# Cross-attention and mixture of experts on one Trainium2 core: raw scores from small products without padded keys, q of two pairs first, and filler products

## The chip, the cores and the metric

The kernel runs on one core of a Trainium2 chip. The metric is the device time of one launch in microseconds; lower is better. All times in this text are in microseconds unless marked ns. Engines: PE is TensorE (PEld its weight loads), DVE is VectorE, ACT is ScalarE, POOL is GpSimd, SP is SyncE, which here issues nearly all DMAs.

## The reference

Sixteen sequences of 256 tokens and width 128 attend to 64 context rows each, with 16 heads of 8. The softmax is unusual: it runs over the heads, not over the keys. Then comes a feed-forward part with two shared experts and eight routed ones, of which each token takes two.

```python
xn = layernorm(x)
q, k, v = xn @ Wq.T, ctx @ Wk.T, ctx @ Wv.T            # 16 heads of 8
scores = einsum('bhqd,bhkd->bhqk', q, k) / sqrt(8)
attn = softmax(scores, axis=1)                          # over the 16 heads
x = x + einsum('bhqk,bhkd->bhqd', attn, v) @ Wo.T
h = layernorm(x)
x = x + h + shared(h) + sum over the top 2 of 8 experts of gate * expert(h)
```

## The kernel before

The 16 sequences are 8 pairs. Attention works in 16 units: unit u is one half (128 queries of each of the two sequences) of pair u // 2. Groups of four units are a body of code (`four_units`), with k = u % 4. The scores of a unit fill four PSUM banks, [128 = 2 sequences x 64 keys, 16 heads x 128 queries]. One unit, engine by engine, each engine in its own program order:

- PE: `raw_scores` (L1337), the products of k and q; then, of earlier units, the output projection (`project_out`, L1368); `minus_max` (L1346), which subtracts the maximum over heads by a product with a negative identity; `weighted_values` of unit u-2 (L1356); then `prologue_rest`, which for the first eight units holds q products (`project_q`, L1309) and transposes (`transposes`, L1298) of later pairs; from unit 9 on transposes for the feed-forward part (L1415).
- DVE: `max_heads` (L922), `sum_heads` of unit u-1 (L927, L930), `low_q` (L860), the addition of the attention result (L934), statistics of the second norm, and at k = 3 the seed of its inverse root (L912 to L917).
- ACT: `exps` (L674), two exponentials for half of the heads each, a copy of the values (L667), and its own `prologue_rest`: first norms (L588), copies of transposes (L594), `high_q` (L600), weights rounded to 16 bits (L565, L572) and scaled (L573), and spreading V (L608).
- POOL: `normalise` (L452), `low_part` (the rests of the rounded weights, L437), `inverse_deviation` (L465), `ffn_inputs` (L476).

Four semaphores tie a unit together: raw_ready, max_ready, s_ready, exp_done. `raw_scores` of the next unit overwrites the banks and so waits for the exponentials, half by half.

Precision: q and k are split into a 16-bit high and low part each. `project_q` makes q of a pair in PSUM, `high_q` and `low_q` write the two parts to `qs`, SyncE stores them to `q_rows` in DRAM (`store_q`, L302) and loads them back spread over the partitions (`load_q`, L314, two DMAs of 64 partitions each for a pair). `kRep` holds, in the same way, both parts of k. In a product over all four combinations of parts a head needs 32 rows.

In this kernel `raw_scores` uses the full array: for each head one product of 128 rows and 128 columns of weights. The weights come from `kPad`, in which all but the head's own rows and the sequence's own keys are zero. GpSimd zeroes kPad once (L403), and SyncE fills it for each pair with 16 DMAs of 8 KB from `kRep` (`pad_k`, L298). kPad has two buffers, so the pad of pair p waits until pair p-2 has been read. The SyncE queue holds in program order: context and x, weight parts 0 to 2, wo (16 small ones), centroids and bias (L317, L318), pad of pair 0 mixed with store and load of q of pairs 0 and 1, weight parts 3 and 4, pad of pair 1, store and load of pairs 2 and 3, then for each further pair a pad, a store and a load, at the end the last two pads.

Ahead of unit 0 stand the q products of pairs 0 to 3. The products of V (`project_v`, L1282) stand behind the raw scores of unit 0, and its copy (L638) in unit 0's ACT code. q of pairs 4 to 7 is made in units 2, 4, 5 and 6 on PE and its low part in units 3, 5, 6 and 7 (`LOW_UNITS`) on DVE. A pair above 3 has bank 7 for its q, so `project_q(pair)` waits for qlo_ready >= pair, the low parts of all pairs below it.

## Time and profile before

| | |
|---|---|
| median of 3 runs | 435.03 us (434.7 to 436.25) |
| the profiled execution's own time | 433.28 us |
| its span, first to last instruction | 431.5 us |
| granted TensorE clock, mean over the span | 0.902 |
| PE / DVE / ACT / POOL busy | 74% / 73% / 65% / 64% |

The attention units take about 32 to 165 us of the span; the feed-forward part follows. A busy share is a mean over parts with different limits. The span leaves out 1.8 us around the first and the last instruction. Granted clock 1.0 is 2.4 GHz, 0.5 is 1.2 GHz.

### The profile page before, as it was taken

How to read it: one execution, taken by the hardware profiler on the slowest of the kernel's cores; microseconds unless marked ns; L12 is line 12 of the kernel's file. 1: busy time of each engine (PE TensorE's matmuls, PEld its weight loads, DVE VectorE, ACT ScalarE, POOL GpSimd, SP SyncE). 2: the span in 40 equal slices, each digit the busy share in tenths (PEclk: the TensorE clock that was granted, in tenths of full speed). 3: DMA queues.
4: the chain of work that ended last, by engine and by line, in shares of the span. 5: the costliest groups of instructions: out<-in, count | busy, mean ns of one | idle time of the engine just before them, and what ended most of it. 6: DMA issues, size and time to landing. Idle time of an engine off the chain costs nothing.

```text
span 431.5 us, 11459 instructions
## 1 busy us (share of the span) xinstructions
PE 319.6 (74%) x3780; PEld 245.9 (57%) x3781; DVE 314.3 (73%) x628; ACT 282.4 (65%) x530; POOL 275.3 (64%) x275
## 2 busy tenths in 40 slices
PE   5456577566767749669887899879999999999400
PEld 1235254344545437347654576669898998989300
DVE  7767778799799995995859856636666666766257
ACT  3675688577578663558876488637676676767265
POOL 8530877589788793077867776606777676777700
PEclk9968599999699875999999899969999999999955
DMA  8838512312300000011111250131323322231087
GB/s 269 277 95 290 153 35 59 81 39 56 82 12 9 2 0 3 0 51 51 46 37 51 82 130 24 46 100 44 99 77 87 91 71 80 73 99 55 8 329 255
DMA packets 37850, 37.18 MB, mean 86 GB/s; under 512 B 13860, under 2 KB 32935, under 8 KB 37296
## 3 DMA queue, kind: packets, MB, share of 16 engines
q1 hardware_dynamic: 33264, 28.18, 22.7%
q0 software_dynamic: 4544, 8.44, 6.0%
q8 instruction: 26, 0.43, 0.4%
q14 instruction: 16, 0.13, 0.1%
HBM read 21.74 MB, written 14.72 MB: 84 GB/s over the span
## 4 chain that ended last, share of the span: by engine, by line
PE 35%; DVE 18%; POOL 15%; issue 14%; SPq 8%; ACT 4%; DMA 4%; POOLq 1%; DVEq 0%; ACTq 0%
SPq L298 5%; POOL E L452 5%; POOL results L532 4%; DVE E L999 4%; PE banks L1543 3%; PE banks L1545 3%; PE banks L1544 3%; PE banks L1558 3%; PE banks L1557 3%; PE banks L1559 2%; PE banks L1475 2%; PE banks L1337 2%; PE banks L1479 2%; PE banks L1477 2%; DVE X L1245 2%
## 5 line engine op out<-in xcount | busy, mean ns | idle before, releaser
L532 POOL DMA_INDIRECT results<-E,qRep x78 | 86.3, 1107 | 44.5 <-issue 27.7
L522 POOL DMA_INDIRECT gathered<-xs,slot x64 | 68.4, 1068 | 41.2 <-issue 18.6
L1216 DVE TENSOR_TENSOR E<-hid,E 128x512 f16<-128x512 f32 x78 | 54.0, 692 | 38.2 <-ACT E L790 37.2
L452 POOL TENSOR_TENSOR E<-E,rZ 128x1024 f32<-128x1024 f32 x32 | 68.3, 2160 | 16.9 <-DVE rZ L930 16.9
L788 ACT ACTIVATE hid<-banks 128x512 f32<-128x512 f32 x78 | 46.8, 601 | 44.0 <-PE banks L1545 25.5
L1475 PE MATMUL banks<-wprojL,E 128*128 128x128 f16 x256 | 46.8, 221 | 15.4 <-DVE E L999 15.3
L750 ACT ACTIVATE hid<-banks 128x512 f32<-128x512 f32 x64 | 38.6, 604 | 29.1 <-PE banks L1461 26.0
L1557 PE MATMUL banks<-wprojL,E 128*128 x312 | 56.1, 219 | 1.8 <-issue 0.9
L999 DVE TENSOR_TENSOR E<-hid,E 128x512 f16<-128x512 f32 x64 | 45.8, 734 | 15.2 <-ACT E L751 14.7
L1559 PE MATMUL banks<-wprojH,E 128*128 x312 | 55.7, 219 | 0.0
L1558 PE MATMUL banks<-wprojH,E 128*128 x312 | 55.7, 219 | 0.0
L674 ACT ACTIVATE E<-banks 128x1024 f32<-128x1024 f32 x32 | 33.1, 1095 | 26.6 <-PE banks L1346 26.6
L922 DVE TENSOR_REDUCE Mx<-banks 128x128 bf16<-128x2048 f32 x16 | 36.7, 2292 | 18.3 <-PE banks L1337 18.3
L790 ACT ACTIVATE E<-banks 128x512 f16<-128x512 f32 x78 | 47.1, 603 | 0.0
L1477 PE MATMUL banks<-wprojH,E 128*128 128x128 f16 x256 | 46.6, 220 | 0.0
L1479 PE MATMUL banks<-wprojH,E 128*128 128x128 f16 x256 | 46.6, 220 | 0.0
L1543 PE MATMUL banks<-qRep,wfcH 128*128 128x256 f16 x156 | 43.6, 280 | 0.5 <-ACT E L790 0.5
L1545 PE MATMUL banks<-qRep,wfcH 128*128 128x256 f16 x156 | 43.5, 279 | 0.0
L1544 PE MATMUL banks<-qRep,wfcL 128*128 128x256 f16 x156 | 43.5, 279 | 0.0
L1475 PEld LDWEIGHTS banks<-wprojL,E 128*128 128x128 f16 x256 | 25.2, 98 | 29.7 <-DVE E L999 24.7
L751 ACT ACTIVATE E<-banks 128x512 f16<-128x512 f32 x64 | 38.4, 601 | 0.0
L927 DVE TENSOR_REDUCE Z<-E 128x128 f32<-128x2048 f32 x16 | 36.4, 2276 | 0.0
(205 smaller groups left out, 833.4 us busy)
## 6 DMA issues: line engine op xcount, KB each, us to landing
qRep<-gathered SPq DMA_DIRECT2D x39, 129.0 KB, 2.2
qRep<-q_rows SPq DMA_DIRECT2D x16, 256.0 KB, 3.9
qRep<-results SPq DMA_DIRECT2D x8, 512.0 KB, 7.0
X<-in_x SPq DMA_DIRECT2D x4, 512.0 KB, 6.3
kPad<-kRep SPq DMA_DIRECT2D x128, 8.0 KB
q_rows<-qRep SPq DMA_DIRECT2D x8, 256.0 KB, 2.3
out<-X SPq DMA_DIRECT2D x8, 256.0 KB, 3.9
xs<-in_wproj_t SPq DMA_DIRECT2D x1, 1536.0 KB, 8.8
```

The lines of the kernel that those rows point to most:

```text
L452: g.tensor_tensor(heads, heads, rZ[:, k % 2, :].unsqueeze(1).unsqueeze(3).broadcast_to([P, HH // 2, P, 2]), ALU.mult).then_inc(attn_ready, 1)
L522: g.indirect_dma_start(out=gathered, out_offset=bass.IndirectOffsetOnAxis(ap=slot[:, k, i:i + 1], axis=0), in_=xs[:, i, :], in_offset=None ...
L532: g.indirect_dma_start(out=results, out_offset=bass.IndirectOffsetOnAxis(ap=xg[:, k, h, 2 * D:ROW].bitcast(I32), axis=0), in_=yg[:, k, h, ...
L999: v.tensor_tensor(hidL[:, i % 2, c], hid[:, c], hidH[:, i % 2, c], ALU.subtract).then_inc(hlo_ready, 1)
L1475: t.matmul(o, hidH[:, e, c, tok], wprojL[:, e, f], start=(e == 0 and c == 0 and q == 0), stop=False, skip_group_check=True)
L1477: t.matmul(o, hidH[:, e, c, tok], wprojH[:, e, f], start=False, stop=False, skip_group_check=True)
L1543: t.matmul(o, wfcH[:, e, f], xgT[:, j, 1], start=True, stop=False)
L1544: t.matmul(o, wfcL[:, e, f], xgT[:, j, 0], start=False, stop=False)
L1545: last = t.matmul(o, wfcH[:, e, f], xgT[:, j, 0], start=False, stop=True)
L1557: t.matmul(o, gH[:, j, c, tok], wprojL[:, e, f], start=(c == 0), stop=False)
L1558: t.matmul(o, gH[:, j, c, tok], wprojH[:, e, f], start=False, stop=False)
L1559: last = t.matmul(o, gL[:, j, c, tok], wprojH[:, e, f], start=False, stop=(c == FC - 1))
```

## The change

1. kPad, its zeroing and all its 128 DMAs go. `raw_scores` takes kRep and qRep directly: for each head and sequence a product of 32 rows and 64 columns of weights, 32 products for a unit instead of 16. A head's 32 rows and the sequence's 64 output partitions select one tile of the array; products for the two sequences alternate. For this, the order of rows in kRep (`select`) and in qRep (`load_q`, now four DMAs of 32 partitions with a stride of 4) changes, and the exponentials read their banks in another order.
2. Only pairs 0 and 1 have their q made ahead of unit 0. Pair u+1 has its q products in unit u (1 to 6), pair u+2 its transposes in unit u (0 to 5), pair u its low part in unit u (2 to 7). Everything from pair 2 on uses banks 6 and 7, with the same waits as pairs above 3 had. On DVE the inverses 2 and 3 go behind the first maximum. On ACT the weight copies are dealt out anew (all four of part 2 in unit 0).
3. The products of V stand ahead of unit 0, into banks 0 and 1, and ACT copies V behind its first four weight copies. PE waits for that copy ahead of unit 0.
4. `keep_going(count)`: products of the identity with itself into a bank part that nobody reads. 20 of them ahead of unit 0, and 6 behind the raw scores of units 0, 1 and 2.

```diff
-            def pad_k(pair, lo=0, hi=PAD_PARTS):
-
-                j = pair % 2
-                if pair > 1:
-                    sp.wait_ge(raw_ready, 2 * pair - 2)
-                for i in range(lo, hi):
-                    r = slice(DK * i, DK * i + DK)
-                    sp.dma_start(kPad[r, j, i % 2, :, i // 2 % 2], kRep[r, pair]).then_inc(kPad_loaded[j], 16)
-
...
-                src = q_rows[pair].rearrange("l (r g) n -> (l r) (g n)", g=QUARTER)
-                for i in range(2):
-                    sp.dma_start(qRep[64 * i:64 * i + 64, pair].rearrange("p g q -> p (g q)"), src
-                                 ).then_inc(q_loaded[pair], 16)
+                for l in range(2):
+                    src = q_rows[pair, l].rearrange("(r g) n -> r (g n)", g=QUARTER)
+                    for i in range(2):
+                        sp.dma_start(qRep[2 * i + l:P:4, pair].rearrange("p g q -> p (g q)"), src
+                                     ).then_inc(q_loaded[pair], 16)
...
-            sp.wait_ge(masks, BASICS + 2)
-            for side in range(2):
-                sp.wait_ge(spread_out[side], 2)
-            pad_k(0, 0, 4)
-            store_q(0, 0)
-            pad_k(0, 4, 6)
-            store_q(0, 1)
-            pad_k(0, 6, 9)
-            load_q(0, 0)
-            pad_k(0, 9)
-            load_q(0, 1)
+            for j in range(2):
+                store_q(0, j)
+            for j in range(2):
+                load_q(0, j)
             for part in range(3, 5):
                 load_weights(part)
...
-            then(g.memset(kPad_flat, 0.0))
...
+            act.wait_ge(masks, BUILT)
+            for i in range(2):
+                act.wait_ge(v_ready, i + 1)
+                s.activation(V[:, 4 * i:4 * i + 4], v_ps[i], ACT.Copy).then_inc(V_ready, 1)
             deviation(1)
+            act.wait_ge(V_ready, 2)
+            spread_v(0, 0)
+            first_norm(2)
...
+                if 0 < u < PAIRS - 1:
+                    high_q(u + 1)
+                if u < PAIRS - 2:
+                    copy_xnT(u + 2)
+                if 0 < u < PAIRS - 3:
+                    first_norm(u + 3)
                 if u == 0:
+                    highs(2, 0, 4)
...
-                    if (first or second) and u in LOW_UNITS:
-                        low_q(4 + LOW_UNITS.index(u))
+                    if second or first and k > 1:
+                        low_q(u)
...
             def project_v():
-                pe.wait_ge(xnT_ready, 4)
+                pe.wait_ge(spread_out[0], 2)
...
+            project_v()
             pe.wait_ge(masks, BUILT)
 
+            def keep_going(count):
+
+                for _ in range(count):
+                    t.matmul(y_ps[:, 0:P], ident[:], ident[:], start=True, stop=True)
+
             def prologue_rest(u):
+                if 0 < u < PAIRS - 1:
+                    project_q(u + 1)
+                if u < PAIRS - 2:
+                    transposes(u + 2)
...
-                for i in range(4):
-                    if not first and i % 2 == 0:
-                        pe.wait_ge(exp_done, 2 * u + i // 2 - 1)
-                    for h in range(4 * i, 4 * i + 4):
-                        at = 2 * (h // 2 % QUARTER) + h // HH
-                        last = t.matmul(scores[:, i, P * (h % 4):P * (h % 4) + P],
-                                        kPad[:, k // 2, h % 2, h // 2].rearrange("p b s -> p (b s)"),
-                                        qRep[:, pair, at, P * (k % 2):P * (k % 2) + P],
-                                        start=(h % 4 == 0), stop=False, skip_group_check=True)
+
+                for i in range(2):
+                    if not first:
+                        pe.wait_ge(exp_done, 2 * u + i - 1)
+                    for odd in range(2):
+                        for g in range(QUARTER):
+                            at = 2 * g + i
+                            for b in range(2):
+                                r = slice(GRP * (2 * b + odd), GRP * (2 * b + odd) + GRP)
+                                last = t.matmul(scores[64 * b:64 * b + 64, 2 * i + odd, P * g:P * g + P],
+                                                kRep[r, pair, QUARTER * i + g],
+                                                qRep[r, pair, at, P * (k % 2):P * (k % 2) + P],
+                                                start=(g == 0), stop=False, skip_group_check=True)
                 last.then_inc(raw_ready, 1)
...
+            pe.wait_ge(V_ready, 2)
...
-                    if first and k == 0:
-                        project_v()
+                    if first and k < 3:
+                        keep_going(6)
...
+            keep_going(20)
             four_units(0, True)
```

## Rows read from the trace of the kernel before

**Rows 1.** Waits: who waited for whom, us in total, times, longest

```profile
PE banks L1337 <- DMA kPad<-kRep: 9.0, 6, 2.3
```

**Rows 2.** Timeline of SyncE's queue: start, duration of the issues, line, count

```profile
15.41 0.43 SPq L318 DMA_DIRECT2D bias<-in_rbias  x1
...
30.35 1.15 SPq L314 DMA_DIRECT2D qRep<-q_rows  x2
...
65.70 12.10 SPq L298 DMA_DIRECT2D kPad<-kRep  x16
...
81.25 12.10 SPq L298 DMA_DIRECT2D kPad<-kRep  x16
```

**Rows 3.** Timeline of TensorE up to unit 0

```profile
14.80 1.95 PE L1309 MATMUL banks<-x,xs 128*64 128x256 f32 x16 [0.82 <-ACT x L594]
...
31.83 1.05 PE L1337 MATMUL banks<-qRep,kPad 128*128 128x128 f16 x16 [2.15 <-DMA kPad<-kRep]
32.72 3.38 PE L1282 MATMUL banks<-xs,x 128*128 128x128 f32 x16
```

**Rows 4.** Timeline of VectorE and TensorE, seed, end of GpSimd's stretch, unit 12

```profile
92.27 0.16 DVE L917 TENSOR_SCALAR rstd<-var 128x8 int32<-128x8 int32 x1
...
110.45 0.61 PE L1415 MATMUL banks<-ident,xs 128*128 128x128 f16 x8 [2.74 <-POOL xs L476]
...
126.49 2.29 DVE L922 TENSOR_REDUCE Mx<-banks 128x128 bf16<-128x2048 f32 x1 [0.42 <-PE banks L1337]
```

**Rows 5.** Timeline of VectorE: start, unit 0, units 6 and 7

```profile
17.42 0.69 DVE L860 TENSOR_TENSOR qRep<-banks,qRep 128x512 f16<-128x512 f32 x1 [0.17 <-ACT qRep L600]
...
35.13 2.49 DVE L855 SCALAR_TENSOR_TENSOR wfcL<-E,wfcH 128x512 f16<-128x512 f32 x4
...
80.24 2.29 DVE L922 TENSOR_REDUCE Mx<-banks 128x128 bf16<-128x2048 f32 x1 [2.40 <-PE banks L1337]
...
85.63 0.63 DVE L860 TENSOR_TENSOR qRep<-banks,qRep 128x512 f16<-128x512 f32 x1
...
88.53 2.29 DVE L922 TENSOR_REDUCE Mx<-banks 128x128 bf16<-128x2048 f32 x1 [0.51 <-PE banks L1337]
```

**Rows 6.** DMA issues: count, KB each, median us from issue to landing

```profile
qRep<-gathered SPq DMA_DIRECT2D x39, 129.0 KB, 2.2
...
q_rows<-qRep SPq DMA_DIRECT2D x8, 256.0 KB, 2.3
```

**Rows 7.** Timeline of ScalarE: weight copies, table, copies of V

```profile
17.28 2.17 ACT L565 ACTIVATE wfcH<-E 128x512 f16<-128x512 f32 x4
...
30.34 1.28 ACT L630 ACT_TABLE_LOAD   x1
...
38.80 1.11 ACT L638 ACTIVATE V<-banks 128x512 f32<-128x512 f32 x2
```

**Rows 8.** Windows, raw products' instructions alone: stretch, length, busy, PEclk, DMA, GB/s

```profile
18.00:20.00 2.00, 0.00 (x0) 0.00 (x0) 0.86 0.33 20
99.70:102.50 2.80, 1.08 (x16) 0.90 (x16) 1.00 0.10 12
```

**Rows 9.** Timeline of TensorE, units 5 to 7

```profile
77.36 0.66 PE L1298 MATMUL banks<-ident,xn 128*128 128x128 f32 x4
...
83.63 1.12 PE L1356 MATMUL banks<-E,vPad 128*32 128x128 f32 x32
86.40 1.08 PE L1309 MATMUL banks<-x,xs 128*64 128x256 f32 x8 [1.65 <-DVE qRep L860]
87.42 1.07 PE L1337 MATMUL banks<-qRep,kPad 128*128 128x128 f16 x16
88.33 1.11 PE L1368 MATMUL banks<-wo,oT 128*128 128x128 f32 x8
```

**Rows 10.** Timeline of TensorE and ScalarE in unit 6: subtraction, exponentials

```profile
82.68 1.02 PE L1346 MATMUL banks<-Mx,negI 128*128 128x512 bf16 x4 [1.53 <-DVE Mx L922]
...
83.37 2.06 ACT L674 ACTIVATE E<-banks 128x1024 f32<-128x1024 f32 x2 [2.12 <-PE banks L1346]
```

More of the change, by code:

```diff
@@ L94, in xattn_moe_kernel @@
         kRep = sb("kRep", [P, PAIRS, HH, SK], F16)
-        kPad = sb("kPad", [P, 2, 2, HH, 2, SK], F16)
+        spare = sb("spare", [P, 2 * ROW + 2 * 12 * TILES], F16)
         vPad = [sb(f"vPad{j}", [P, 2, HH * (GRP + DK)]) for j in range(2)]
@@ L135, in xattn_moe_kernel @@
         table = sb("table", [P, 2, -(-MAX_TILES // QUAD) * QUAD], I32)
-        kPad_flat = kPad[:].rearrange("p j o g b s -> p (j o g b s)")
-        padding = kPad_flat[:, 0:2 * ROW].rearrange("p (s r) -> p s r", s=2)
+        padding = spare[:, 0:2 * ROW].rearrange("p (s r) -> p s r", s=2)
         x2_flat = x2[:].rearrange("p l t -> p (l t)")
@@ L191, in xattn_moe_kernel @@
         k_ps = [banks[:, i, :] for i in (0, 1)]
-        v_ps = [banks[:, i, :] for i in (4, 5)]
+        v_ps = [banks[:, i, :] for i in (0, 1)]
         spread_ps = [[banks[:, 2 * i:2 * i + 2, :] for i in sides] for sides in ((1, 3), (0, 1))]
@@ L195, in xattn_moe_kernel @@
         q_ps = [banks[:, i, :] for i in (6, 7)]
-        t_in = [t_ps[0], t_ps[1], t_ps[0], t_ps[1]] + 4 * [banks[:, 6, :]]
-        q_in = [q_ps[0], q_ps[1], q_ps[0], q_ps[1]] + 4 * [banks[:, 7, :]]
+        t_in = t_ps + (PAIRS - 2) * [banks[:, 6, :]]
+        q_in = q_ps + (PAIRS - 2) * [banks[:, 7, :]]
         scores = banks[:, 0:4, :]
@@ L226, in xattn_moe_kernel @@
             sem(n) for n in ("xn_ready", "xn1_ready", "t_ready", "xnT_ready", "q_ready"))
-        kPad_loaded, vPad_ready = [sem(f"kPad_loaded{j}") for j in range(2)], sem("vPad_ready")
+        vPad_ready = sem("vPad_ready")
         raw_ready, max_ready, s_ready = sem("raw_ready"), sem("max_ready"), sem("s_ready")
@@ L674, in exps @@
                     s.activation(E[:, k, 4 * i:4 * i + 4].rearrange("p g q o -> p g o q"),
-                                 scores[:, 2 * i:2 * i + 2].rearrange("p b (g o q) -> p (b g) o q", o=2, q=P), ACT.Exp,
+                                 scores[:, 2 * i:2 * i + 2].rearrange("p o (g q) -> p g o q", q=P), ACT.Exp,
                                  scale=DK ** -0.5).then_inc(exp_done, 1)
@@ L820, in _ @@
             for low in range(2):
-                m = select[:, low].rearrange("p g (s i b x) -> p g s i b x", s=2, i=2, b=2)
+                m = select[:, low].rearrange("p g (b x s i) -> p g b x s i", s=2, i=2, b=2)
                 for i in range(2):
-                    last = v.tensor_copy(m[:, :, low, i], groups)
+                    last = v.tensor_copy(m[:, :, :, :, low, i], groups)
             last.then_inc(select_ready, 1)
@@ L886, in _ @@
             first_stats(3)
-            inverse(2)
-            inverse(3)
-            for pair in range(2, 4):
-                low_q(pair)
             def pair_stats(n, j):
@@ L1290, in transposes @@
                 pe.wait_ge((xn_ready, xn1_ready)[pair % 2], pair // 2 + 1)
-                if pair in (2, 3):
-                    pe.wait_ge(xnT_ready, pair - 1)
-                if pair == 4:
-                    pe.wait_ge(qlo_ready, 3)
-                if pair > 4:
+                if pair == 2:
+                    pe.wait_ge(qlo_ready, 1)
+                if pair > 2:
                     pe.wait_ge(xnT_ready, pair)
@@ L1302, in project_q @@
                 pe.wait_ge(xnT_ready, pair + 1)
-                if pair in (2, 3):
-                    pe.wait_ge(qlo_ready, pair - 1)
-                if pair > 3:
+                if pair > 1:
                     pe.wait_ge(qlo_ready, pair)
```

63 lines of the change are left out of this document (8 added, 55 removed).

## The prediction

> **What bounds the kernel now.** I read the page first, then the waits, then one timeline per engine over the 16 attention units, then the chain of waits around the places where an engine stood idle. Behind 165 us everything hangs on the end of attention, so I look only at how fast the units follow each other. A unit is a loop over three engines: 16 raw products on TensorE, a maximum on VectorE, four products that subtract it, two exponentials on ScalarE that free the scores' banks. Nothing of it is near full; each engine waits for the next. Two things hold it up besides. TensorE waits for kPad six times, 9.0 us [rows 1]: SyncE spends 12.1 us on the 16 small issues of one pair, and the following block begins 15.55 us behind it [rows 2]; the rest is the store and load of a later pair's q in the same queue. A pair of units can't be quicker than that. The first unit begins at 31.83 us, right behind the last pad of pair 0 [rows 3]. Later GpSimd holds: from the seed of the second norm (92.27 us) its stream runs almost without a gap through norm steps, two normalisations and four weight rests to the lower halves of pair 0, and TensorE has waited 2.74 us for these when it goes on at 110.45 us [rows 4].
>
> **The first unit.** What stays: the products of q end at 16.75 us [rows 3], its low half of pair 1 at 18.11 us [rows 5], SyncE is free at 15.84 us [rows 2]. So the stores go out at about 17.3 and 18.2 us. A store lands in 2.3 us [rows 6]; bulk loads still run, I take 20.0 us. The four loads of pair 0 take 4 x 0.58 us of SyncE (half of what one pair's two took, 1.15 us), to 22.3 us, and a load of their size lands in 2.2 us [rows 6]: 24.5 us. TensorE: the products of V move up to 16.75 us, 1.7 us at full clock (they took 3.38 us at the low one [rows 3]). ScalarE can copy V only behind its four weight copies, 19.45 us, and needs 1.1 us [rows 7]: 20.6 us. Then come the 20 products nobody reads. Each is as large as one of V's eight, which took 3.38/8 = 0.42 us at the low clock: 0.21 us at the full one, 4.3 us together, or 8.5 us if all run low. TensorE was idle from 16.75 us, and the granted clock, 0.86 over 18 to 20 us, had fallen before 20 [rows 8]; now it works until 18.4 us, and I take the clock as high or coming up soon: raw products at 25.5 us (25.1 if high at once, 26.7 if the first eight are slow). The later of the two, TensorE, sets it. ScalarE must not be late: its table load, now the last thing ahead of unit 0, ended at 31.6 us [rows 7]; 1.7 us come ahead of it (copies of V, the first spreading), four copies of 0.6 us of q and of transposes go behind, and so do about 1.9 us of waits for TensorE between them: about 29.1 us. The first exponential is due at 25.5 + 1.15 + 2.29 + 0.69 and the handoffs, 29.7 us, so this is hidden, by 0.6 us only. Gain at this point 31.83 - 25.5 = 6.3 us.
>
> **A raw product's new price.** 32 products of 128 columns by 32 rows and 64 keys stand for 16 full ones. If the two halves of the array run side by side, the time stays at 1.07 us [rows 9]. That products of 64 output rows run two by two, q shows: four of them with 256 columns each take 1.08 us, while V's eight at full width with 128 columns, 1024 columns as well, took 3.38 us at the low clock, 1.7 us at the full one [rows 3, 9]. And 32 records of products of 32 output rows take 1.12 us [rows 9]. The bound from below is no change (the same columns stream), from above twice, 2.0 us: either the pairs go one by one, or load and product of a tile stand in line (16 products 1.08 us and 16 loads 0.90 us [rows 8]). I take 1.15 us, by the nearest row (1.12) plus a new change of shape between transposes and raw products: raw products start 0.06 us before the q products end, but the full products of L1368, which have the shape that the raw ones had, start 0.16 us before those end [rows 9]. So about 0.1 us for a change.
>
> **Units 0 to 7.** The raw products of unit 0 end at 26.65. Maximum 2.29, subtraction to the last exponential 2.75 (0.69 until the first of the two starts, and 2.06 for both [rows 10]), then the second half of the raw products 0.6, and four handoffs: unit 1 ends its raw products at 32.5. VectorE has by then done both moved inverses (four small operations, about 0.8) and the four weight rests (2.5 [rows 5]). Six fillers, 1.3 us, lie under the 2.29 us maximum; if the clock were low they would be 2.6 us and stick out by 0.3. Unit 1: maximum to 34.8, subtraction, q of pair 2 (1.08), transposes (0.66 [rows 9]), raw products to 38.5; VectorE's sum and reciprocal end there too.
> From unit 2 on comes what I think most readers would overlook: all q share bank 7, and the low half of pair u is now made in unit u, behind maximum, sum and reciprocal, while TensorE's stream has the products of pair u+1, the transposes of pair u+2 and the raw products of unit u+1 queued behind the wait for it. Before, only units 5 and 6 had this. Unit 6 prices it: maximum at 80.24, low half 85.63, q products 86.40, raw 87.42, next maximum 88.53 [rows 5, 9]: 8.3 us, with transposes 8.9, and with the raw price of above 8.35 and 8.95. A unit without it takes about 6 to 7. Maximum 2 starts at 38.5, so does its low half at 43.9 and maximum 3 at 47.4; three units of 8.95 and one of 8.35 lead to maximum 7 at 82.7 us. It was at 88.53 [rows 5]. So of the 6.3 us 5.8 are left: all of SyncE's stalls go, and the new wait takes nearly as much back. The q of pairs 2 to 7 are needed two units or more behind their low half, some 9 us and more against 2.3 + 2.3 + 2.2 us of store, issues and load: hidden.
> Nothing else costs: ScalarE's copies per unit are under 8 us, GpSimd's normalisation and rests 6.5 us, the 3.6 us memset and SyncE's waits that go were covered.
>
> **Units 8 to 15.** The stretch from the seed to 110.45 us is GpSimd's own work, 18.2 us, and moves as it is: 5.8 us earlier. In unit 12 a wait for kPad goes, but VectorE idled only 0.42 us there [rows 4]: -0.4. Five raw products on the path (10 to 13, 15) cost 5 x 0.1 = +0.5. The rest, 165 us to the end, shifts.
> Sum: -5.8 - 0.4 + 0.5 = -5.7 us. The profiled execution has 433.28 us with a span of 431.5, and its own after would be 427.6; the median of the three runs is 435.03, so I say 429.3 us.
>
> **Rivals.** (A) Products of two halves don't overlap, or tile loads stand in line. For it: no row has 32-row tiles; against: all rows with column tiles overlap. 0.9 us more than 1.07 in 13 raw products on the path, instead of 0.1: +10.4 us, 439.7. The gain without any raw cost is 6.2 us and some units hide theirs; over 13 raw products it is gone at 0.5 us each. Chance 0.10. This one ends slower.
> The Trainium skill (TensorE: Matmul & The Clock Gate, Part 3: Packing small matmuls) says that a weight load overlaps running products only where the row groups differ. In this change a tile's next load has its own row group, which would give rival A's in-line price; the full-width raw products, one row group all of them, hid their loads here, so the trace doesn't bear the rule out for them, and no run yet shows small tiles.
> (B) The fillers run at the low clock or q lands late: raw products at 28.5 to 29.4 us, 3 to 3.9 us of the gain gone, 432.8. For it: the clock was low by 20 us, and V's products at 32.72 us were slow too [rows 3, 8]. Chance 0.11.
> (C) The clock falls in units 3 to 7, where TensorE has more gaps and no fillers: subtraction, q products, transposes and raw products take up to twice their 1.0, 1.1, 0.7 and 1.1 us, as V's did [rows 3], some 3 us per unit, five units: +15, 444. Against: units 5 and 6 had these gaps and the fast prices [rows 9]. Chance 0.05.
> (D) More gain: GpSimd's stretch shortens because the 1.1 us VectorE stall in the seed doesn't come, TensorE stays fast behind 110 us (its raw, subtraction and value products were slow there, 1 to 2.5 us), or the first unit is at 24.5. -9 us, 426. Chance 0.14.
> My forecast has 0.57, its own range 427 to 431.8; 0.03 is for what I don't see.
>
> **Numbers.** A measurement tells about 0.5% (2.2 us) from no change. Faster by more: 0.57 + 0.14 and 0.03 of B = 0.74. Within: the rest of B and the near side of others, 0.11. Slower: A and C, 0.15. The range 425.0 to 435.0 takes in forecast, B and most of D; A and C lie outside.
>
> **What would show it.** Right: first raw products at 25 to 27 us; they take 1.1 to 1.2 us; no idle time there behind a DMA; q products of units 2 to 6 released by the low half, 8.3 to 9 us between maxima; seed at about 86.5 us and the 18.2 us behind it unchanged. Wrong: raw products near 2 us, a first unit at 29, q products at twice their price in units 3 to 7, or a seed stretch that got shorter.

## The result, and the profile of the changed kernel

The changed kernel takes 428.31 us (median of 4 runs, 428.15 to 429.16), the kernel before 435.18 beside it (4 runs, 434.7 to 436.25): a ratio of 0.9843 with an interval of 0.982 to 0.9865. The profiled execution took 428.38 us with a span of 426.6; before it was 433.28 and 431.5. The forecast was 429.3, in a range of 425.0 to 435.0, faster with a chance of 0.74. It came true, and in the attention part by nearly the forecast amount (5.6 us instead of 5.7), but some of its terms were off and cancelled, which is luck. The rows show which. All ratios leave out slow executions (one of the kernel before with 438.82 us, one of a later kernel with 549.3 us at a mean granted clock of 0.558).

The timeline of SyncE's queue ahead of unit 0 (start, duration of the issues, line, count):

```profile
17.53 1.24 SPq L290 DMA_DIRECT2D q_rows<-qRep  x2
21.91 5.50 SPq L303 DMA_DIRECT2D qRep<-q_rows  x8
```

The view of the two stores' line over 15 to 30 us; its last row says how long a store took to land:

```profile
L290 SPq DMA_DIRECT2D q_rows<-qRep x2: 377/378/378, 17.5 to 18.4; - x2
...
DMA to landing us min/median/max: 3.8/4.1/4.4
```

The timeline of TensorE, up to unit 0 (against [rows 3]), then unit 2 with the raw products of unit 3, then units 5 and 6 (against [rows 9]), then the end of GpSimd's stretch (against [rows 4]):

```profile
16.94 2.05 PE L1237 MATMUL banks<-xs,x 128*128 128x128 f32 x16
20.83 4.70 PE L1276 MATMUL banks<-ident 128*128 128x128 f32 x40 [1.84 <-ACT V L596]
26.77 0.67 PE L1294 MATMUL banks<-qRep,kRep 32*64 32x128 f16 x32 [1.24 <-DMA qRep<-q_rows]
...
46.31 1.97 PE L1260 MATMUL banks<-x,xs 128*64 128x256 f32 x8 [0.57 <-DVE qRep L817]
48.21 1.12 PE L1251 MATMUL banks<-ident,xn 128*128 128x128 f32 x4
49.26 1.08 PE L1294 MATMUL banks<-qRep,kRep 32*64 32x128 f16 x32
...
73.60 1.08 PE L1260 MATMUL banks<-x,xs 128*64 128x256 f32 x8 [1.73 <-DVE qRep L817]
74.62 0.66 PE L1251 MATMUL banks<-ident,xn 128*128 128x128 f32 x4
75.20 0.67 PE L1294 MATMUL banks<-qRep,kRep 32*64 32x128 f16 x32
...
82.11 1.08 PE L1260 MATMUL banks<-x,xs 128*64 128x256 f32 x8 [1.65 <-DVE qRep L817]
83.12 0.67 PE L1294 MATMUL banks<-qRep,kRep 32*64 32x128 f16 x32
...
106.09 0.61 PE L1372 MATMUL banks<-ident,xs 128*128 128x128 f16 x8 [2.64 <-POOL xs L449]
```

The timeline of VectorE in unit 1, then in unit 6 with the maximum of unit 7 (against [rows 5]), and the seed:

```profile
33.16 2.29 DVE L875 TENSOR_REDUCE Mx<-banks 128x128 bf16<-128x2048 f32 x1 [0.32 <-PE banks L1294]
35.36 0.64 DVE L892 CAST centH<-cent 128x8 f16<-128x8 f32 x1
36.04 1.08 DVE L894 TENSOR_TENSOR centL<-cent,centH 128x8 f16<-128x8 f32 x1
37.04 2.27 DVE L880 TENSOR_REDUCE Z<-E 128x128 f32<-128x2048 f32 x1
39.35 0.95 DVE L883 RECIPROCAL rZ<-Z 128x128 f32<-128x128 f32 x1
40.22 2.23 DVE L875 TENSOR_REDUCE Mx<-banks 128x128 bf16<-128x2048 f32 x1
...
75.94 2.29 DVE L875 TENSOR_REDUCE Mx<-banks 128x128 bf16<-128x2048 f32 x1 [0.85 <-PE banks L1294]
78.15 2.28 DVE L880 TENSOR_REDUCE Z<-E 128x128 f32<-128x2048 f32 x1
80.46 0.95 DVE L883 RECIPROCAL rZ<-Z 128x128 f32<-128x128 f32 x1
81.33 0.63 DVE L817 TENSOR_TENSOR qRep<-banks,qRep 128x512 f16<-128x512 f32 x1
...
83.86 2.29 DVE L875 TENSOR_REDUCE Mx<-banks 128x128 bf16<-128x2048 f32 x1
...
87.96 0.16 DVE L870 TENSOR_SCALAR rstd<-var 128x8 int32<-128x8 int32 x1
```

Three things are to be seen. The first raw products come 5.1 us earlier than before, and what they wait for is a DMA, not TensorE: the products nobody reads (40 records for 20 of them) end at 25.5 us, and q lands 1.2 us later. The raw products of a unit take 0.67 us instead of 1.07. And from unit 2 on a unit is a straight chain with no slack in it. The waits over 20 to 170 us have its new link, and no kPad any more:

```profile
PE banks L1260 <- DVE qRep L817: 7.2, 5, 1.7
```

In the rows of unit 6 above the links follow one another without a gap: maximum, sum, reciprocal and low half on VectorE (75.94 to 81.96), then q products (in units 2 to 5 transposes too) and raw products on TensorE (82.11 to 83.79), then the next maximum at 83.86. That is 7.9 us in unit 6, and 8.5 us in each of units 3 to 5.

### The profile page after: what moved, and what is told of

Read it like the earlier page. It is cut to its first block, busy times and chain, and to the rows that moved or that the text cites. A ratio compares the mean times of both kernels' runs of the same rounds, so it can differ in the third digit from the quotient of the medians.

```text
span 426.6 us, 12009 instructions
## 1 busy us (share of the span) xinstructions
PE 322.9 (76%) x4112; PEld 249.0 (58%) x4113; DVE 311.8 (73%) x628; ACT 282.2 (66%) x530; POOL 270.3 (63%) x274
## 4 chain that ended last, share of the span: by engine, by line
PE 38%; DVE 22%; issue 16%; POOL 13%; DMA 5%; ACT 4%; SPq 1%; POOLq 1%; DVEq 0%; ACTq 0%
DVE Z L880 5%; POOL results L505 5%; POOL E L425 4%; PE banks L1516 3%; PE banks L1515 3%; PE banks L1501 3%; PE banks L1502 3%; PE banks L1503 3%; PE banks L1433 3%; PE banks L1517 3%; DVE E L954 2%; PE banks L1435 2%; PE banks L1437 2%; DVE Mx L875 2%; PE banks L1417 2%
## 5 line engine op out<-in xcount | busy, mean ns | idle before, releaser
L495 POOL DMA_INDIRECT gathered<-xs,slot x64 | 66.7, 1042 | 43.9 <-issue 18.6
L1433 PE MATMUL banks<-wprojL,E 128*128 128x128 f16 x256 | 48.2, 225 | 13.5 <-DVE E L954 13.4
L1435 PE MATMUL banks<-wprojH,E 128*128 128x128 f16 x256 | 48.1, 224 | 0.0
L1437 PE MATMUL banks<-wprojH,E 128*128 128x128 f16 x256 | 48.0, 224 | 0.0
```

The costliest lines, as they stand in the source:

```text
L495: g.indirect_dma_start(out=gathered, out_offset=bass.IndirectOffsetOnAxis(ap=slot[:, k, i:i + 1], axis=0), in_=xs[:, i, :], in_offset=None ...
L1433: t.matmul(o, hidH[:, e, c, tok], wprojL[:, e, f], start=(e == 0 and c == 0 and q == 0), stop=False, skip_group_check=True)
L1435: t.matmul(o, hidH[:, e, c, tok], wprojH[:, e, f], start=False, stop=False, skip_group_check=True)
L1437: last_product = t.matmul(o, hidL[:, e, c, tok], wprojH[:, e, f], start=False, stop=(e == 1 and c == FC - 1), skip_group_check=True)
```

## The experiments

I kept three theories for where the gain comes from. The first: it is the raw products straight from kRep, by their price and by the pads that go, and the other parts give nothing in the end, since what they win at the start is paid back by the wait for the one q bank. The second: the early start (q, V, fillers) is a gain of its own. The third: the clock, kept up by the fillers, is the gain. Beside these stood the question why a raw product costs less than any row of before said.

Four moments tell more than whole times, since the rest of the kernel follows them: the first raw products, maximum 3, the seed of the second norm, and the last addition of the attention result. In the batch of the first four runs the part behind the last addition was some 80 us longer in every trace, and the kernel before took 521.02 us too; why isn't known. Of these runs I read the attention part and the ratio.

| kernel | first raw | maximum 3 | seed | last addition | median us | ratio (interval) |
|---|---|---|---|---|---|---|
| before | 31.83 | 56.23 | 92.27 | 174.49 | 435.18 | 1 |
| after | 26.77 | 50.43 | 87.96 | 168.88 | 428.31 | 0.9843 (0.982 to 0.9865) |
| after, again | 26.76 | 48.64 | 86.17 | 167.93 | 427.35 | 0.9847 (0.980 to 0.9894) |
| no fillers | 26.31 | 49.52 | 87.07 | 168.88 | 512.35 | 0.9877 (0.9787 to 0.9967) |
| raw products alone | 28.81 | 53.92 | 87.48 | 168.55 | 510.66 | 0.9812 (0.9739 to 0.9885) |
| raw products alone, again | 29.65 | 54.74 | 88.30 | 170.03 | 428.76 | 0.9873 (0.9834 to 0.9912) |
| q behind raw scores | 26.61 | 48.04 | 83.75 | 164.72 | 507.32 | 0.9757 (0.9679 to 0.9834) |
| q behind raw scores, again | 26.58 | 47.99 | 83.76 | 164.97 | 424.75 | 0.9781 (0.9724 to 0.9838) |
| weight copies first too | 26.77 | 46.69 | 81.64 | 163.50 | 421.92 | 0.9702 (0.9662 to 0.9742) |
| the same without fillers | 28.06 | 50.20 | 82.92 | 164.88 | 423.33 | 0.9719 (0.9672 to 0.9766) |
| raw products 0.69 us longer | 27.23 | 50.51 | 90.12 | 172.76 | 432.48 | 0.9956 (0.993 to 0.9982) |

The kernel before took 521.02 us beside the first batch (the rows above 500 us), 435.12 beside the two repetitions of after and of raw products alone and the kernel with the weight copies first, and 434.47 beside the other three.

**No fillers.** The changed kernel without `keep_going`.

```diff
-            keep_going(20)
             four_units(0, True)
...
-                    if first and k < 3:
-                        keep_going(6)
```

> The changed kernel without any of its 38 filler products. My theory: the first unit is set by the landing of q (26.77 us), not by the 20 fillers (they ended at 25.5), so it begins at the same time; but TensorE then comes out of 7 us of idleness at the low clock, and the subtractions, q products, transposes and raw products of units 0 and 1 take up to twice as long. Maximum 3 starts 2 to 4 us later, the whole is +2 to +4 us, 430.3 to 432.3. Rival 1: the fillers buy nothing, the clock comes back by itself within unit 0: within 1 us of the changed kernel. Rival 2: they are the whole gain: 435.

Measured: ratio 0.9877, last addition at 168.88, against 168.88 and 167.93 in the two traces of the changed kernel. The fillers do what they are for: windows of the changed kernel, then of this one (stretch, length, busy time and instructions of PE, PEld, DVE, ACT, POOL, granted clock, DMA share, GB/s):

```profile
24.00:28.00 4.00, 2.76 (x51) 2.48 (x51) 2.33 (x16) 3.98 (x9) 1.79 (x2) 1.00 0.65 190
```

```profile
24.00:28.00 4.00, 1.09 (x32) 0.88 (x32) 2.35 (x16) 3.98 (x8) 1.81 (x2) 0.50 0.66 205
```

TensorE stood idle for 7.3 us ahead of these raw products, the clock was at its lower level (1.2 GHz), and they took 1.09 us instead of 0.67. But the last addition shows nothing of it that is clear of the difference between two traces of one kernel (0.95 us), and my own 2 to 4 us didn't come. The gain is there without fillers, so the third theory falls for this kernel; an effect of a microsecond either way isn't excluded.

**Raw products alone.** The kernel before, with only the new raw products and what they need (order of rows in kRep and qRep, no kPad, no pads, no memset). q of four pairs stays ahead of unit 0, V behind it, no fillers.

```diff
-            def pad_k(pair, lo=0, hi=PAD_PARTS):
...
-                                        kPad[:, k // 2, h % 2, h // 2].rearrange("p b s -> p (b s)"),
-                                        qRep[:, pair, at, P * (k % 2):P * (k % 2) + P],
+                                last = t.matmul(scores[64 * b:64 * b + 64, 2 * i + odd, P * g:P * g + P],
+                                                kRep[r, pair, QUARTER * i + g],
+                                                qRep[r, pair, at, P * (k % 2):P * (k % 2) + P],
```

> The kernel before with one part of the change: small raw products straight from kRep, no kPad, its DMAs and waits gone. The order of q (pairs 0 to 3 ahead of unit 0), the place of V and no fillers are as before. My theory (the small products and the SyncE queue are the gain, and q late in one bank gives much of it back): unit 0 begins at about 29.7 us, behind q of pair 3, 3 us later than in the changed kernel, but units 3 and 4 take 6.5 to 7 us instead of 8.5; the seed of the second norm comes at 86 to 88 us, about as in the changed kernel (87.96) or up to 2 us earlier: 426 to 429. Rival (q first and the fillers are what pays): 431 to 433.

Measured: ratio 0.9812 and, in the repetition, 0.9873; last addition at 168.55 and 170.03 (the latter in its slowest execution, 431.67 us). Both intervals overlap that of the whole change. It starts 2.0 us later than the changed kernel and has caught up by the seed (87.48 against 87.96), since its units 3 and 4 don't wait for a q bank: its maxima 3 to 5 stand at 53.92, 60.17 and 66.95, 6.3 and 6.8 us apart, where the changed kernel needs 8.5. Units 5 and 6 take 8.5 and 7.9 us here too. It loses time in unit 2, which takes 11.8 us (42.16 to 53.92; 8.6 in the kernel before): the raw products stand behind q products of pair 4, and these behind the values, which wait for GpSimd:

```profile
49.83 1.08 PE L1337 MATMUL banks<-E,vPad 128*32 128x128 f32 x16 [1.00 <-POOL E L430]
```

In the repetition it doesn't quite catch up: seed and last addition are each 2.1 us behind those of the changed kernel in the same batch. This bears out the first theory against the second in the main: raw products alone have most of the gain or all of it, and what the other parts add is between nothing and 2 us.

**One tile after another.** The same 32 products, but all four of a tile one behind another, instead of sequences in turn.

```diff
-                        for g in range(QUARTER):
-                            at = 2 * g + i
-                            for b in range(2):
+                        for b in range(2):
+                            for g in range(QUARTER):
+                                at = 2 * g + i
```

> The changed kernel with its 32 raw products in another order: the sequence outside, the head group inside, so that four products in a row use one tile of the array. They took 0.67 us with the two sequences alternating. Theory A (a product of 128 columns keeps its tile busy for the 53 ns that its columns need, and products on different tiles run side by side when they are next to each other in the stream): 32 x 0.053 + 0.2 = 1.9 us, less where one tile's last product overlaps the next tile's first; the whole +6 to +12 us. Theory B (a product on a small tile takes about 29 ns, and pairs ran one by one at 15 ns): stays 0.67 us. Theory C (small products wait in queues of their tiles, so four tiles ran at once, also over a distance of 8 in the stream): stays 0.67 to 0.9 us. B and C leave the time as it is.

Measured (one execution): raw products 0.69 us instead of 0.67, last addition at 168.81. The order hardly matters with four in a row.

**q behind the raw scores.** The chain above has the q products between low half and raw products, though the raw products don't need them. Here `prologue_rest` of a unit stands behind the raw scores of the next one.

```diff
+                    if 0 < u <= 2 * 4:
+                        prologue_rest(u - 1)
                     if first and k < 3:
                         keep_going(6)
...
-                    if u < 2 * 4:
-                        prologue_rest(u)
```

> The changed kernel with q products and transposes moved on TensorE alone: those of unit u now stand behind the raw scores of unit u+1, under the maximum, instead of ahead of them. Nothing else moves. My theory (in units 2 to 6 the raw scores stand behind q products that wait for the low half in the one bank of q, 8.5 us between maxima): the wait of 1.65 us goes, and the 1.7 us of products lie under the 2.3 us maximum, so a unit takes 6.9 to 7.3 us; GpSimd with about 7.2 us per unit in units 4 to 7 bounds it next: seed at 80 to 83 us instead of 87.96, the whole 5 to 8 us faster, 420 to 423. Rival (the wait only moves: q products, transposes and the output projection, 2.9 us together, now delay the subtraction, and GpSimd takes the rest): at most 2 us faster, 426 to 429.

> The changed kernel with q products and transposes behind the next raw scores alone, once more for its time. In its first trace the last addition of attention stood at 164.72 us, 4.2 us ahead of the changed kernel's. All theories: 423 to 424.5 us, between the changed kernel (427.35) and the one with both moves (421.9).

Measured: ratio 0.9757 and 0.9781, last addition at 164.72 and 164.97, 3 to 4 us earlier than in the changed kernel. So the wait for the bank, with the 1.7 us of products behind it, did cost that much where it stood. The units don't fall to the 6.9 to 7.3 us that I expected, though; they take 7.6 to 8.3. The timeline of ScalarE in the first of the two shows what comes next:

```profile
65.17 0.60 ACT L573 ACTIVATE qRep<-banks 128x512 f16<-128x512 f32 x1 [1.29 <-PE banks L1260]
65.75 0.60 ACT L567 ACTIVATE x<-banks 128x512 f32<-128x512 f32 x1
66.37 1.65 ACT L561 ACTIVATE xn<-X,shift,rstd 128x128 f32<-128x128 f32 x4
67.92 0.61 ACT L545 ACTIVATE wprojH<-xs 128x512 f16<-128x512 f32 x1
68.44 0.61 ACT L546 ACTIVATE xs<-xs 128x512 f32<-128x512 f32 x1
68.96 2.01 ACT L631 ACTIVATE E<-banks 128x1024 f32<-128x1024 f32 x2
```

ScalarE stands 1.29 us waiting for q, has the norm and two weight copies queued behind that wait, and the exponentials behind those, at 68.96 us. The subtraction for the first of them had ended by about 67 us (its four products start at 66.53 and take 1.04).

**Weight copies first.** As above, and on ScalarE the copies that need no q go ahead of `high_q`, so that the wait is filled.

```diff
+                for part, e in WEIGHT_UNITS[u]:
+                    high_and_scaled(part, e)
                 if 0 < u < PAIRS - 1:
                     high_q(u + 1)
...
-                for part, e in WEIGHT_UNITS[u]:
-                    high_and_scaled(part, e)
```

> The changed kernel with two moves: q products and transposes on TensorE behind the next raw scores, as in the experiment with that alone, and on ScalarE the weight copies of a unit ahead of the copies of q and transposes instead of behind them. With the first move alone a unit took 7.6 to 8.3 us between maxima, and the chain ran through ScalarE, which waited 1.3 us for TensorE's q products and then had norm, weights and spreading ahead of the next exponentials. My theory (ScalarE is the next bound): weights fill that wait, units 2 to 6 take 7.0 to 7.4 us, the seed stands at 80.5 to 82 us (87.96 in the changed kernel, 83.75 with the first move), the last addition at 161.5 to 163, the whole 420 to 422.5 us. Rival (GpSimd or VectorE is the next bound already): as with the first move alone, seed 83 to 84 us, last addition 164 to 165, whole 423.5 to 425.

Measured: 421.92 us, ratio 0.9702, the fastest of all. Its timeline of TensorE has a wait that, of the others, only the same version without fillers has (0.69 us there), and the timeline of SyncE shows the round trip behind it:

```profile
54.48 0.67 PE L1294 MATMUL banks<-qRep,kRep 32*64 32x128 f16 x32 [3.08 <-DMA qRep<-q_rows]
```

```profile
46.80 0.38 SPq L290 DMA_DIRECT2D q_rows<-qRep  x1
48.97 3.52 SPq L303 DMA_DIRECT2D qRep<-q_rows  x4
```

From the store of q of pair 2 to the first product that reads it is 7.7 us, of which 3.1 are now a wait. I would expect this version to be faster without it, but didn't try to make that q earlier. In the changed kernel these transfers were hidden by the slow units. From the seed on, GpSimd is the limit here as before: TensorE goes on 18.2 us behind the seed (99.81 us) and has waited 2.35 us for it (the timeline of GpSimd in the same run; the normalisation and the rests come a second time between the second row and the third):

```profile
85.69 4.22 POOL L425 TENSOR_TENSOR E<-E,rZ 128x1024 f32<-128x1024 f32 x2
89.86 2.30 POOL L410 TENSOR_TENSOR wprojL<-x,wprojH 128x512 f16<-128x512 f32 x2
...
98.53 1.14 POOL L449 TENSOR_TENSOR xs<-xn,xs 128x512 f16<-128x512 f32 x1
```

**The same without fillers.** Same edit as in the first experiment, on this version, to see whether faster units make the clock matter.

> The kernel with both moves (q products behind the next raw scores, weight copies first; 421.9 us) without its 38 filler products. Without them the changed kernel's attention ended at the same time (168.88 us). My theory: fillers buy nothing here either: within 1.5 us, 420.5 to 423.5. Rival (with shorter units TensorE's early clock counts): 2 us or more slower.

Measured: 423.33 us, ratio 0.9719; last addition 1.4 us later. But q landed later in this execution: the first raw products waited for the DMA until 28.06 us, 1.3 us later than with fillers, and TensorE doesn't set that moment. The intervals overlap too: this may be a small gain of the fillers, or none. It isn't settled.

**Longer raw products.** Eight full products into a bank part that the next raw products overwrite, between the two halves of a unit's raw products. How much of a raw price reaches the end?

```diff
+                    if i:
+                        for _ in range(8):
+                            t.matmul(scores[:, 2, 0:P], ident16[:], ident16[:], start=True, stop=True)
```

> The changed kernel with 8 full products nobody reads ahead of the second half of every unit's raw products, into a bank that this half then overwrites: 8 x 0.053 us and a change of shape, so that the raw products end about 0.5 us later, as in the kernel before. It asks how much of the gain is that raw products take 0.67 instead of 1.07 us, and how much is kPad's stalls on SyncE. My theory: some 12 raw products lie on the path, so it is 4 to 6 us slower than the changed kernel and nearly all of the gain is gone: 432 to 434, the last addition of attention at 172 to 174.5 us (167.9 to 168.9 in the changed kernel, 174.5 before). Rival (SyncE's stalls are the gain, the products' length is covered by VectorE and GpSimd): at most 2 us slower, 429, last addition by 170.5.

The timeline of TensorE in unit 4:

```profile
58.27 0.43 PE L1297 MATMUL banks<-qRep,kRep 32*64 32x128 f16 x16
58.64 0.62 PE L1291 MATMUL banks<-ident 128*128 128x128 f16 x8
59.19 0.44 PE L1297 MATMUL banks<-qRep,kRep 32*64 32x128 f16 x16
```

From 58.27 to 59.63 is 1.36 us, 0.69 more than 0.67. Measured: ratio 0.9956 against 0.9843 to 0.9847, that is 4.7 to 4.9 us of 434.47 (the intervals leave about 2 us to either side); last addition 3.9 to 4.8 us later. So some six or seven of the 16 raw products reach the end with their price; in units 3 to 6 each does (9.2 us between maxima in unit 3, against 8.5). By that I estimate that the 0.40 us between 1.07 and 0.67 gave about 2.6 us. The other 3 us of the 5.6 would then be the pads and the waits for them; that is what is left over, no run takes the pads away alone.

**What a small product costs.** Two kernels, executed once each, with 32 products of each kind ahead of unit 0, none of which is read. The first:

```diff
+            for _ in range(32):
+                t.matmul(y_ps[0:64, 0:P], ident16[0:32, 0:64], ident16[0:32, :], start=True, stop=True)
+            for i in range(32):
+                b = i % 2
+                t.matmul(y_ps[64 * b:64 * b + 64, 0:P], ident16[64 * b:64 * b + 32, 0:64],
+                         ident16[64 * b:64 * b + 32, :], start=True, stop=True)
...
+            for _ in range(32):
+                t.matmul(y_ps[0:64, 0:P], ident16[:, 0:64], ident16[:], start=True, stop=True)
+            for _ in range(32):
+                t.matmul(y_ps[:, 0:P], ident16[:], ident16[:], start=True, stop=True)
```

> The changed kernel with five more groups of 32 products nobody reads behind its first 20, each product with 128 columns of 16 bits: 32 rows by 64 on one tile; the same on two tiles in turn; 32 rows by 128; 128 rows by 64; the full 128 by 128. Theory B (a product on a small tile takes less time than 128 columns need): the first group takes about 0.7 us, as the raw products did. Theory C (they wait in queues of their tiles, and different tiles overlap far apart in the stream): the first group takes 32 x 0.053 + 0.2 = 1.9 us, the second 1.07, the other three 1.9 us each. The full group should take 1.9 us by either. Theory B and the number of rows as the cause: 32 by 128 is short too, 128 by 64 is not; the number of output rows as the cause: the other way round. The whole time isn't the question here (later by 5 to 9 us, as the first unit starts that much later).

Its timeline of TensorE (the first row is the bulk of the first group; its last two start one by one up to 28.10 us):

```profile
26.35 1.86 PE L1379 MATMUL banks<-ident 32*64 32x128 f16 x30
28.00 0.24 PE L1382 MATMUL banks<-ident 32*64 32x128 f16 x1
...
28.13 1.08 PE L1382 MATMUL banks<-ident 32*64 32x128 f16 x30
29.14 1.96 PE L1384 MATMUL banks<-ident 32*128 32x128 f16 x32
31.03 3.58 PE L1386 MATMUL banks<-ident 128*64 128x128 f16 x32
34.54 1.96 PE L1388 MATMUL banks<-ident 128*128 128x128 f16 x32
36.43 0.67 PE L1294 MATMUL banks<-qRep,kRep 32*64 32x128 f16 x32
```

The second, with four tiles (rows, bank, half): four in turn, then each eight times in a row, then two tiles that differ in rows but share their output half, then products of 128 rows on the two halves in turn.

```diff
+            for i in range(32):
+                small(*((0, 5, 0), (2, 5, 1), (1, 4, 0), (3, 4, 1))[i % 4])
+            for i in range(32):
+                small(*((0, 5, 0), (2, 5, 1), (1, 4, 0), (3, 4, 1))[i // 8])
+            for i in range(32):
+                small(*((0, 5, 0), (1, 4, 0))[i % 2])
+            for i in range(32):
+                b = i % 2
+                t.matmul(y_ps[64 * b:64 * b + 64, 0:P], ident16[:, 0:64], ident16[:], start=True, stop=True)
```

> The changed kernel with four groups of 32 products nobody reads, 128 columns of 16 bits each, behind the first 20. One tile of 32 rows by 64 took 53 ns per product, two tiles (other rows, other output rows) about 30. Group 1, four tiles in turn as in the raw scores: 0.67 us. Group 2, the same four tiles with eight products in a row on each: if products wait in their tile's queue while later ones on other tiles go ahead in the array, still about 0.67 us; if only neighbours overlap, near 1.9 us. Group 3, two tiles with different rows and the same output rows (two banks) in turn: 1.07 us if rows alone make tiles independent, 1.9 us if two tiles with the same outputs exclude each other. Group 4, products of 128 rows by 64 in turn on both halves of the output rows: alone on one half they took 109 ns each, where I had expected 53; in turn 1.9 us for the 32 (59 ns each) if the surplus is a load that stands behind its own tile's product.

Its windows over the line of the small products (a product that runs across an edge counts on both sides), cut where the groups change:

```profile
25.72:26.18 0.46, 0.46 (x32) 0.46 (x33) 1.00 0.67 178
26.18:27.17 0.99, 0.99 (x44) 0.99 (x33) 1.00 0.68 215
27.17:28.10 0.93, 0.93 (x42) 0.93 (x37) 1.00 0.74 207
```

and from its timeline the last group:

```profile
28.19 1.08 PE L1391 MATMUL banks<-ident 128*64 128x128 f16 x32
```

Time for one product of 128 columns, by the starts of the groups and their 32 products: one tile alone 56 ns (26.35 to 28.10, 31 steps), 32 rows at full width 59 ns (29.14 to 31.03), full size 59 ns (34.54 to 36.43), two tiles on different halves 34 ns (28.13 to 29.14, 30 products), two tiles on one half with different rows 29 ns (0.93 us), four tiles in turn 14 ns (0.46 us), each eight times in a row 31 ns (0.99 us). The 59 and the 34 hold the edges of their groups: by the starts of the single products inside them, a full product too follows every 56 ns, and the two tiles on different halves, of which one ran behind the other at the end, start a product every 28 ns (27 steps in 0.75 us, from 28.13 to 28.89). So each tile takes a product every 56 ns, whatever its neighbours do, and all four tiles run side by side, as long as the next tile's product isn't too far behind in the stream: four in a row still go at nearly full rate (0.69 us for a unit), eight in a row don't.

How far is too far can be read from single starts. With eight in a row, the next tile's first product starts at 26.42 us, ahead of the last three of the tile before it (26.47, 26.53 and 26.58), and so at each of the three changes of tile. The row at 28.00 us above is of this kind: the second group's first product, ahead of the last two of the first group (28.05 and 28.10). So here products on different tiles don't start in the order of the stream. That the depth of some queue is the cause of the limit is a guess.

**Repetitions.** The changed kernel and the one with raw products alone again, in one batch with the kernel that has the weight copies first.

> The changed kernel itself once more, so that it stands beside the others on one chip. All theories: 0.984 of the kernel before, and the last addition of attention at 168.9 us of its span.

> The raw products alone once more (no kPad; order of q, place of V and no fillers as before). In its first trace the last addition of attention stood at 168.55 us, against 168.88 in the changed kernel and 174.49 before. My theory (this part is the whole gain): equal to the changed kernel within 1 us, 427 to 429.5. Rival (the whole time gets something from the other parts that the attention part of the trace doesn't show): 431 or more.

Measured: 0.9847 and 0.9873, as in the table. The first has a different unit 2. The clock falls to its lower level in both traces of the changed kernel, in each behind the same 2.30 us in which TensorE waited for the maximum, but not for equally long. Windows of the changed kernel as first profiled, and of the repetition:

```profile
43.80:50.60 6.80, 6.02 (x77) 3.51 (x69) 2.50 (x4) 3.72 (x7) 5.71 (x4) 0.50 0.21 67
```

```profile
42.90:46.30 3.40, 3.17 (x37) 1.53 (x35) 3.21 (x3) 2.24 (x3) 2.30 (x2) 0.50 0.00 0
```

In the first the lower clock covers the q products, transposes and raw products of this unit; in the second it has passed when they start at 46.29 us, and fell on the subtraction and the values, which VectorE's stream hides. They took 1.08, 0.66 and 0.67 us there instead of 1.97, 1.12 and 1.08, and maximum 3 came at 48.64 instead of 50.43. At the last addition 0.95 us of the 1.8 are left. In the two kernels with groups of small products ahead of unit 0 the same wait of 2.3 us was followed by no fall at all.

## Why the prediction was right, and where its terms were off

**The start.** Forecast 25.5 us, set by the fillers; measured 26.77, set by q. TensorE's side was right (its stream reached the end of the fillers at 25.5). The store was costed at 2.3 us from the median of a whole kernel's stores [rows 6]; here it took 3.8 and 4.4 us, against a median of 2.1 over the program; that the bulk loads beside them are the cause is argued, no run takes them away. The allowance for them (stores landed at 20.0 us) was 1.9 us too small, and four issues took 2.8 us instead of 2.3. Loss of gain 1.3 us.

**The raw price.** Forecast 1.15 us with a floor of 1.07, "the same columns stream". Measured 0.67. This is the step that was mis-sized beyond its bounds: the lower bound supposed that only the two halves of the output overlap, but products with different rows overlap as well, so four run at once. Rival A, in which the price rises, is out; one small tile by itself takes a product every 56 ns, as the full array does, so no load stands in line there. The rule of the Trainium skill (TensorE: Matmul & The Clock Gate, Part 3: Packing small matmuls) by which a load overlaps only where the row groups differ is therefore not borne out for small tiles; in one shape, below, something like it shows. The term for five raw products on the path (+0.5) is replaced by a gain.

**Units 2 to 6.** The wait for the one q bank was the right mechanism, and its price is right: 8.95 us less 0.48 for the raw products gives 8.47, measured 8.5 between maxima in units 3 to 5; unit 6 8.35 less 0.48 gives 7.87, measured 7.92. Unit 2 took 10.2 us (40.22 to 50.43), 1.3 more than forecast, since the clock was at its lower level (0.50 from 43.8 to 50.6 us, windows above) and q products, transposes and raw products took 4.0 us together; in the repetition they took 2.3 and the unit 8.4. Rival C had the mechanism right, but for one unit, and whether it costs anything depends on when the fall ends. Moving the q products behind the raw scores gave 3 to 4 us back, which is the price of this wait and of the products behind it, as far as the next limit lets it be seen.

**Unit 1.** It took 7.1 us between maxima instead of 6.0. I had VectorE free to take maximum 2 as soon as the raw products were there; in fact two operations on the centroids (0.64 and 1.08 us, in the timeline above) stand between its maximum and its sum. In the kernel before the same two took 0.16 and 0.17 us, at a time when GpSimd was idle; here GpSimd was at work beside them. Whether that is the cause wasn't tested. Its own stream, without a gap, set the start of maximum 2: the raw products were ready at 38.8, the maximum began at 40.22.

**Maximum 7** came at 83.86 instead of 82.7, 1.2 us late. The lateness by maxima: 0.9 us at maximum 0, 0.7 at 1, 1.7 at 2 (the centroids), 3.0 at 3 (the clock), and the four units behind it won 1.9 back.

**Behind the seed.** Forecast: unchanged, +0.1 us. From seed to the products that wait for GpSimd it was 18.1 us (18.2 forecast), and with the smaller raw price the whole stretch to the last addition is 80.9 us instead of 82.2, 1.3 us less. The forecast had five raw products here as each costing; with the price falling they won some of it, and by the longer raw products six or seven of all 16 count, not 13 as the working for rival A had it. All of the 1.3 us is won by maximum 12 (-0.5 at maximum 10, -1.0 at 11, -1.3 at 12), so the raw products of units 13 and 15, which the forecast counted, are covered. The wait for kPad in unit 12 (forecast -0.4) is in it and can't be told apart.

**The sum.** Seed -4.3 us (forecast -5.8), behind it -1.3 (forecast +0.1): -5.6 at the last addition, forecast -5.7. Two errors of more than a microsecond cancel: that the total came out is luck. The span moved by 4.9 us, the medians by 6.9; executions of the kernel before lay between 432.23 and 436.96 us in one batch, so I read nothing into that difference.

**Where the gain went.** Of the 5 us by which the first unit is earlier, 2 to 3 come with the raw products alone (28.81 and 29.65 us). The other parts lead by 3.5 us at maximum 3, 6.1 in the repetition, and the wait for the q bank takes 4.0 us of it back in units 3 and 4: at the end they have no lead that the intervals bear out (427.35 and 428.76 us in one batch, ratios 0.9847 and 0.9873; last addition 168.88 against 168.55 in the first traces, 167.93 against 170.03 in the second). What was argued ahead (the wait "takes nearly as much back") is now seen from both sides, by leaving q-first out and by moving the wait.

## What to carry to other kernels

When work is moved out of a start into a loop, follow every wait that it brings into an in-order stream: the same q products cost 3 to 4 us more ahead of the raw scores than behind them, and on ScalarE whatever can run without the result belongs ahead of the instruction that waits. Price a change in two halves, each alone: here one half held nearly the whole gain, and the other could be turned from little or nothing into a further 5.4 us (427.35 to 421.92) by two changes of order. A duration that is a median over a program is not that of its busiest moment: take the row of the same moment.

## What the runs showed of the hardware that I had not expected

Products on separate 32-row, 64-column tiles run four at once, at 14 ns for 128 columns each, and may stand up to four in a row of one tile with hardly a loss (0.69 us for 32, against 0.67). A product on another tile started ahead of up to three earlier ones that still waited for theirs. A product of 128 rows and 64 columns whose next one is on the same half takes 110 ns (31.03 to 34.54, 32 of them), though one of full width takes 59 over its whole group; with the halves in turn it takes 32 (28.19 to 29.21). So a half-width product of full height seems not to hide its load behind its own half, while smaller ones and full ones do. The clock's fall in unit 2 began at 43.8 us in one trace of the changed kernel and lasted 6.8 us, and at 42.9 us in another and lasted 3.4 us, behind the same work; it moved maximum 3 by 1.8 us. A forecast to better than a microsecond isn't to be had there.
